# A graph network's second edge pass: ten steps of look-ahead, gathers gated by copy and scores; relation MLP with another order on TensorE

## What is computed

```
# layer 0, the relation MLP: for every edge
he = edge_attr @ edge_fc_W + edge_fc_b
t  = relu(einsum('ed,mdf->emf', he, rel_att_W1) + rel_att_b1)
g  = sigmoid(einsum('emf,mf->em', t, rel_att_W2) + rel_att_b2)

# layer 1, the second edge pass: src, dst per edge
e = tanh((X @ Wq)[src] + (X @ Wk)[dst])
scores = e @ Wphi
exp_scores = exp(scores - max(scores))
alpha = exp_scores / (segment_sum(exp_scores, src) + 1e-9)
msg = alpha * ((X @ Wy_w + Wy_b)[dst] + e @ We)
out = segment_sum(msg, src)
x = layernorm(x + out)
```

## Time and profile before

| | |
|---|---|
| median of the timed runs | 3582.48 us (3579.48 to 3582.94, 3 runs) |
| profiled execution | 3547.52 us, span 3545.2 us |
| granted TensorE clock, mean | 0.796 of full speed |
| busy share of the span: PE, DVE, POOL, ACT | 75%, 51%, 47%, 44% |
| relation MLP | 97 to about 669 us |
| first edge pass (unchanged) | about 800 to 1900 us |
| second edge pass: first gather, first and last `take` | 2084.5 us, 2142.2 us, 3471.5 us |

### The profile page before, as it was taken

One profiled execution on the slowest core, in us unless ns is written; L12 is line 12 of the kernel. 1 busy time (PEld: TensorE's weight loads), 2 busy tenths in 40 slices (PEclk: granted clock), 3 DMA queues, 4 the chain that ended last, 5 costly groups with the idle time before them and its releaser, 6 DMA issues. The chain is left out here.

```text
span 3545.2 us, 70863 instructions
## 1 busy us (share of the span) xinstructions
PE 2645.4 (75%) x17372; PEld 1828.1 (52%) x17372; DVE 1795.3 (51%) x5675; ACT 1560.4 (44%) x4560; POOL 1679.9 (47%) x1723
## 2 busy tenths in 40 slices
PE   5899999699877788887889545566666666676664
PEld 4343333277655566666667424455455455554552
DVE  8934531155433343334345625565565566565664
ACT  2677777455433333333335114344443444444442
POOL 0344444311356566655650035655656556666550
PEclk9999999889888778778779657766777767667775
DMA  8233333255433333333331022222222222222220
GB/s 96 90 100 98 98 108 110 65 180 147 137 107 104 97 99 102 99 101 98 102 95 60 14 68 59 66 63 62 70 62 67 65 62 66 66 67 67 63 59 18
DMA packets 321789, 297.77 MB, mean 84 GB/s; under 512 B 196992, under 2 KB 249237, under 8 KB 321680
## 3 DMA queue, kind: packets, MB, share of 16 engines
q0 software_dynamic: 72320, 160.26, 16.0%
q1 hardware_dynamic: 249360, 136.30, 13.9%
HBM read 191.89 MB, written 25.22 MB: 61 GB/s over the span
## 5 line engine op out<-in xcount | busy, mean ns | idle before, releaser
L1553 POOL DMA_INDIRECT sum_acc<-kv_table,rec_all x784 | 804.2, 1026 | 555.2 <-issue 207.5
L1043 POOL DMA_INDIRECT area_b<-h_table,src_g x544 | 559.8, 1029 | 370.6 <-remote 135.0
L1613 PE MATMUL bank<-sum_acc,probT 128*128 128x193 f32 x1760 | 506.8, 451 | 108.8 <-DVE probT L1741 57.8
L1613 PEld LDWEIGHTS bank<-sum_acc,probT 128*128 128x128 f32 x1760 | 416.2, 264 | 168.1 <-DVE probT L1741 89.6
L1113 PE MATMUL bank<-hs,y_sb 128*128 128x129 f32 x2400 | 415.9, 329 | 67.3 <-ACT y_sb L1136 64.5
L1113 PEld LDWEIGHTS bank<-hs,y_sb 128*128 128x128 f32 x2400 | 381.8, 241 | 79.6 <-ACT y_sb L1136 76.1
L501 POOL DMA_INDIRECT early<-h_table,src_g x240 | 236.9, 987 | 373.0 <-ACT sum_acc L707 290.3
L1140 ACT COPY y_sb<-bank 128x512 f32<-128x512 f32 x300 | 175.4, 585 | 520.1 <-PE bank L1104 282.9
L1227 DVE SCALAR_TENSOR_TENSOR sum_acc<-sum_acc,shrink,bank 128x129 f32 x300 | 104.7, 349 | 569.8 <-remote 266.6
L707 ACT ACTIVATE sum_acc<-bank,bias 128x512 f32<-128x512 f32 x588 | 351.4, 695 | 38.3 <-PE bank L585 30.9
L585 PE MATMUL bank<-area_b,wc 64*128 64x512 f32 x1176 | 362.1, 631 | 4.2 <-issue 3.7
(11 more groups left out here) (287 smaller groups left out, 4561.1 us busy)
## 6 DMA issues: line engine op xcount, KB each, us to landing
hs<-area_b SPq DMA_DIRECT2D x300, 258.0 KB
area_b<-in_edge_attr SPq DMA_DIRECT2D x97, 256.0 KB, 2.7
rows_table<-early POOLq DMA_DIRECT2D x60, 258.0 KB
area_b<-rows_table POOLq DMA_DIRECT2D x60, 258.0 KB
sum_acc<-kv_table,rec_all POOLq DMA_INDIRECT x784
qb<-q_table SPq DMA_DIRECT2D x220, 48.0 KB
area_b<-h_table,src_g POOLq DMA_INDIRECT x544
hbT<-hT_table SPq DMA_DIRECT2D x300, 16.0 KB
```

The costliest lines, as they stand in the source:

```text
L1043: pool.indirect_dma_start(out=landed_rows[:, k * GT + j, 0:D], out_offset=None, in_=h_table, in_offset=bass.IndirectOffsetOnAxis(ap=src_g[ ...
L1553: pool.indirect_dma_start(out=landed_rows[:, g % RING1 * GT + j, :], out_offset=None, in_=kv_table, in_offset=bass.IndirectOffsetOnAxis(ap ...
L1613: last = pe.matmul(bank[4 + k % 2][0:BN, 0:KV + 1], probT_v[:, k % 2, j, :], row_v[:, k % RING, j, AD:RK], start=(j == 0), stop=(j == GT - 1))
```

## The change

In the relation MLP `hidden(o)` becomes `hidden(o, m)`, a third of it, and PE and ACT take another order. In the second pass the look-aheads grow from 4 steps to 10, rings grow from 5 to 10 places (the rows of the ring now lie in three old buffers), two PSUM banks each take the transposes and the queries, and the four gathers of a group are issued in two pairs with a gate each. `SU` is 10, `PT` 5, `RING1` 8 as before. The core of the diff:

```diff
-RING = 5
+RING = 10
+PT = 5
...
-                    def hidden(o):
-                        pe.wait_ge(ea_sb, o + 1)
-                        for n in range(2 * M):
-                            m, half = n // 2, n % 2
+                    def hidden(o, m):
+                        if m == 0:
+                            pe.wait_ge(ea_sb, o + 1)
+                        for n in (2 * m, 2 * m + 1):
+                            half = n % 2
...
                     for o in range(OCTS):
-                        if o + 2 < OCTS:
-                            turn(o + 2)
                         if o + 1 < OCTS:
-                            hidden(o + 1)
+                            hidden(o + 1, 0)
+                            hidden(o + 1, 1)
+                        if o % 2:
+                            logits(o)
+                        elif o + 3 < OCTS:
+                            turn(o + 3)
+                        if o + 1 < OCTS:
+                            hidden(o + 1, 2)
+                        if o % 2 and o + 3 < OCTS:
+                            turn(o + 3)
                         if o >= TILE and o % TILE == 0:
                             turn_logits(o // TILE - 1)
-                        if o % 2:
-                            logits(o)
...
                     for o in range(OCTS):
-                        if o + 2 < OCTS:
-                            turned(o + 2)
                         if o >= TILE and o % TILE == 0:
                             keep_logits(o // TILE - 1)
                         if o + 1 < OCTS:
-                            rectified(o + 1)
+                            rectified(o + 1, (0, 1))
+                        if o % 2 == 0 and o + 3 < OCTS:
+                            turned(o + 3)
+                        if o + 1 < OCTS:
+                            rectified(o + 1, (2,))
+                        if o % 2 and o + 3 < OCTS:
+                            turned(o + 3)
...
-            row_v = area_a[:, 0:RING * GT * RK].rearrange("p (u j c) -> p u j c", u=RING, j=GT)
+            homes = [(area_a, RING1 * GT * KV + n * GT * RK) for n in range(6)] + [(x_words, n * GT * RK) for n in range(3)] + [(h_words, 0)]
+            row_v = [home[:, at:at + GT * RK].rearrange("p (j c) -> p j c", j=GT) for home, at in homes]
+            query_bank, hot_bank = (bank[0], bank[7]), (bank[1], bank[6])
...
                     def body(s, k, edge):
-                        if inside(edge, k, RING):
+                        if inside(edge, k, 7):
...
-                            sp.wait_ge(stepped, n + 1)
+                            sp.wait_ge(sum_done, n + 1)
                             load_step(s1, k1, g, b)
...
-                    pool.memset(row_v[:, :, :, KV + AD:RK], 1.0).then_inc(cleared, 1)
+                    for row in row_v:
+                        pool.memset(row[:, :, KV + AD:RK], 1.0).then_inc(cleared, 1)
...
-                            pool.wait_ge(stepped, last_step + SU + 1)
-                        gather(g)
+                            pool.wait_ge(moved, last_step + 1)
+                        gather(g, 0)
+                        if g >= RING1:
+                            pool.wait_ge(score_done, last_step + 1)
+                        gather(g, 1)
...
                     def body(s, k, edge):
-                        if inside(edge, k, 1):
-                            share_top(*step_of(s, k, 1))
                         if inside(edge, k, 3):
-                            queries(*step_of(s, k, 3))
-                        if inside(edge, k, 4):
-                            turn(*step_of(s, k, 4))
-                        if inside(edge, k, 2):
-                            turn_max(*step_of(s, k, 2))
+                            share_top(*step_of(s, k, 3))
+                        if inside(edge, k, 7):
+                            queries(*step_of(s, k, 7))
+                        if inside(edge, k, 9):
+                            turn(*step_of(s, k, 9))
                         if inside(edge, k, 1):
                             messages(*step_of(s, k, 1))
-                    rounds(pe, body, 4)
+                        if inside(edge, k, 5):
+                            turn_max(*step_of(s, k, 5))
+                    rounds(pe, body, 9)
...
                     def body(s, k, edge):
-                        if inside(edge, k, 3):
-                            move_rows(*step_of(s, k, 3))
                         if inside(edge, k, 2):
-                            tanh(*step_of(s, k, 2))
-                        if inside(edge, k, 4):
-                            squared(*step_of(s, k, 4))
-                        if inside(edge, k, 1):
-                            exponentials(*step_of(s, k, 1))
-                        if inside(edge, k, 4):
-                            turned(*step_of(s, k, 4))
-                    rounds(act, body, 4)
+                            exponentials(*step_of(s, k, 2))
+                        if inside(edge, k, 8):
+                            turned(*step_of(s, k, 8))
+                        if inside(edge, k, 6):
+                            tanh(*step_of(s, k, 6))
+                        if inside(edge, k, 7):
+                            move_rows(*step_of(s, k, 7))
+                        if inside(edge, k, 10):
+                            squared(*step_of(s, k, 10))
+                    rounds(act, body, 10)
...
                     def body(s, k, edge):
+                        if inside(edge, k, 6):
+                            add_queries(*step_of(s, k, 6))
+                        if inside(edge, k, 4):
+                            highest(*step_of(s, k, 4))
+                        if inside(edge, k, 9):
+                            outside(*step_of(s, k, 9))
+                        if inside(edge, k, 10):
+                            hot(*step_of(s, k, 10))
+                        if inside(edge, k, 6):
+                            score(*step_of(s, k, 6))
                         if inside(edge, k, 2):
-                            add_queries(*step_of(s, k, 2))
-                        if inside(edge, k, 3):
-                            outside(*step_of(s, k, 3))
-                        if inside(edge, k, 4):
-                            hot(*step_of(s, k, 4))
-                        if inside(edge, k, 1):
-                            highest(*step_of(s, k, 1))
-                        if inside(edge, k, 2):
-                            score(*step_of(s, k, 2))
-                        if inside(edge, k, 1):
-                            spread_p(*step_of(s, k, 1))
+                            spread_p(*step_of(s, k, 2))
                         if inside(edge, k, 0):
                             take(s, k)
-                    rounds(v, body, 4)
+                    rounds(v, body, 10)
```

More of the change, by code:

```diff
@@ L699, in keep_logits, with rectified @@
                         act.activation(logit, bank[5][:, :], ACT.Identity, bias=bias2[:, 0:1]).then_inc(logit_sb, 1)
-                    def rectified(o):
-                        if o >= 3:
+                    def rectified(o, pairs):
+                        if o >= 3 and 0 in pairs:
                             act.wait_ge(logit_ps, (o - 3) // 2 + 1)
-                        for n in range(2 * M):
+                        for n in range(2 * pairs[0], 2 * pairs[-1] + 2):
                             m = n // 2
@@ L725, in _ @@
                     turned(1)
-                    rectified(0)
+                    rectified(0, (0, 1, 2))
+                    turned(2)
                     for o in range(OCTS):
-                        if o + 2 < OCTS:
-                            turned(o + 2)
                         if o >= TILE and o % TILE == 0:
@@ L1541, in body, with gather @@
                             tell(s, k)
-                    sp.wait_ge(cleared, 1)
-                    rounds(sp, body, RING)
+                    sp.wait_ge(cleared, RING)
+                    rounds(sp, body, 7)
                 @block.gpsimd
                 def _(pool):
-                    pool.memset(row_v[:, :, :, KV + AD:RK], 1.0).then_inc(cleared, 1)
+                    for row in row_v:
+                        pool.memset(row[:, :, KV + AD:RK], 1.0).then_inc(cleared, 1)
                     pool.memset(acc_st, 0.0).then_inc(cleared, 1)
                     pool.memset(top_st, NONE).then_inc(cleared, 1)
-                    def gather(g):
+                    def gather(g, pair):
                         pool.sem_inc(ticks, 1)
-                        for j in range(GT):
+                        for j in (2 * pair, 2 * pair + 1):
                             pool.indirect_dma_start(
@@ L1578, in turn @@
                         n = s * SU + k
-                        if not is_first(n):
-                            pe.wait_ge(hotT_done, n)
+                        into = hot_bank[k % 2][0:BN, :].bitcast(BF16)
+                        pe.wait_ge(hotT_done, n + 1)
```

(4 more changed lines are left out.)

92 lines of the change are left out of this document (51 added, 41 removed).

## The result

The changed kernel takes 3630.54 us (median of four runs, 3625.8 to 3637.05), beside 3582.71 us for the kernel before on the same chip (3579.48 to 3584.41): ratio 1.0147, interval 1.012 to 1.0174. It is 48 us slower. The forecast was 204 us faster: 3378 us, in a range of 3280 to 3495 us. The measured time lies 135 us above that range.

A forecast was written before the change was run, and what follows sets the result against it. The prediction took PE's late hand-over during gather chains as the second pass's bound. Steps -195, clearings +3 and MLP -12 gave -204 us: 3378 us as median from 3582.5, range 3280 to 3495 us.

The forecast's parts named there:

- What bounds the step: Second edge pass: PE's results are announced late while POOL chains gathers, making a step 6.07 us.
- rival 1: Second pass: lateness wholly hidden, POOL gathers without pause, 4.73 us per step, 3280 us in all; chance 0.17.
- the gates stay shut and the chain ends: Second pass: when PE is held, ACT and DVE soon have nothing to copy or score, so POOL's gathers stop.
- rival 3: Second pass: gates open earlier, POOL never pauses for PE, 7.05 us per step, +215 us, 3780 us; chance 0.08.
- the pace by a chain of four: Second pass: four gathers, 5.3 us, pace 196 of 220 steps; 5.18 us per step on average, -195 us.
- Rival 4: Second pass: no effect, lateness grows with the look-ahead, 6.05 us per step, within 0.2%; chance 0.03.
- the other terms: Outside the second pass's steps: +3 us for more clearings of ones columns on POOL, -12 us for the relation MLP.
- Fill: Start of the second pass: three more short bodies, some 9 us, offset by a shorter end; counted 0, up to 10 us either way.
- what is queued behind a late load: SP in the second pass: `tell`, on which `move_rows` waits, has a 10 us window against 7.5 us lateness; counted 0.
- MLP: Relation MLP: ACT idles 2.59 us, not 2.72, per pair, and logit turns fall behind its work; -12 us, bounds 0 and -60.
- Gathers beside DVE: Second pass: denser DVE work lengthens gathers, mean over median from 79 to some 92 ns; -184 us instead of -195.
- the clock: PE in the second pass: denser work keeps PE at the upper clock level more often; no size given.

The follow-up runs named there:

- gate on PE: The changed kernel with its gathers also waiting for PE's queries and messages: 3491.08 us where before took 3570.28, one run each; 0.9903 where before took 2952.6.
- old gate: The changed kernel with all four gathers of a group waiting again for PE's messages: 2923.53 us, ratio 0.9898, where before took 2951.89 us.
- new gate: The kernel before with only the gathers' waits changed to ACT's copy and DVE's scores: 2954.68 us, ratio 1.0005, where before took 2951.89 us.
- MLP part alone: The kernel before with only the new order of PE's and ACT's work in the relation MLP: 2923.51 us, ratio 0.9908.

## Why the prediction was wrong, by its steps

**What bounds the step: right for this chip, taken for a property of the kernel.** The late hand-over of PE during a chain of gathers is what the first chip shows, before and after. Five other chips don't show it. There the step is POOL's own 4.63 to 4.71 us, which is the step of rival 1 (4.73), but rings and gates are worth nothing, since the kernel before is at that floor too.

**The step that failed: "the gates stay shut and the chain ends".** This was the argument that kept rival 3 at 0.08, and the pace by a chain of four (5.18 us) rests on it: after four gathers POOL was to wait for the next score. But each score opens the gate for four more gathers, DVE's steps are 4.1 us apart, and four gathers take 5.1 us, so the next gate is open before the four are out. DVE makes that score from PE results of the body before, and the chain doesn't end until DVE has used up what it has. In the stall above the scores end at 2899.39 and 2903.57 us (`lane_max`), which let out the gathers from 2900.18 and from 2905.30 us, eight in one chain:

```profile
2899.31 0.08 DVE L1762 DVE_READ_ACCUMULATOR2_ANT lane_max<- 128x1 f32 x1
...
2903.49 0.08 DVE L1762 DVE_READ_ACCUMULATOR2_ANT lane_max<- 128x1 f32 x1
...
2905.30 0.95 POOL L1573 DMA_INDIRECT sum_acc<-kv_table,rec_all  x1 [0.30 <-issue]
```

DVE stops at 2905.2 us and waits for PE until 2911.98. So the forecast's argument isn't false in itself, DVE does run dry, but too late: the gate for four more gathers was opened 1.6 us before. PE's first gap comes only at 2906.2 us. It is so in most chains of eight and more behind the fill, 64 in all: in 37 of them no score ends after PE's first unexplained gap over 0.9 us, in 3 there is no such gap, and in 24 DVE goes on to score while PE is held. The chains grew from four and eight to eight and twelve, and the wait for PE with them. In the kernel before, the gate waited for PE's own messages, and I read it as a brake, though a loose one (39 chains of eight): POOL could not go far where PE was held. It was taken away in the same edit that gave the slack to hide lateness. It is rival 3 in kind, and in size 6.34 us, not 7.05: the loop of two bodies meets its lateness in one step of three (74 of 219), not in each.

What the runs show of this: chains, steps and waits in the three traces of chips that hold PE, and that beside the gate on PE, in one run, the chains are shorter and the step is 5.78 us. What they don't show: the old gate and the new gate each alone there. So that one run puts the brake, with the look-ahead kept, at 0.56 us per step; how much of the loss comes from the gates and how much from the rings stays open.

Two slips in the forecast's numbers changed nothing of this. Rival 3's own terms give 3582.5 + 215 + 3 - 12 = 3788 us and not 3780. Rival 4's 6.05 us per step is 4 us for the pass, and with the 9 us of the other terms 0.4%, not "within 0.2%".

**Fill, counted 0, was +36 us.** The forecast saw that SP has to be seven bodies ahead and named `tell` as what is queued behind a late load, and priced it at nothing. In the fill ACT's first copy came at 2122.14 us, when the 32 gathers' chain was over, and what it waited for is SP's `tell` (L1549). SP's loads of records and q rows and ACT's copy in the timeline:

```profile
2091.30 0.01 SPq L1543 DMA_DIRECT2D qb<-q_table  x1
2100.49 0.71 SPq L1542 DMA_DIRECT2D rec_sb<-rec  x1
2104.69 0.70 SPq L1543 DMA_DIRECT2D qb<-q_table  x1
2120.79 0.00 SPq L1542 DMA_DIRECT2D rec_sb<-rec  x1
2120.89 0.33 SPq L1543 DMA_DIRECT2D qb<-q_table  x1
2122.14 0.83 ACT L1668 COPY sum_acc<-sum_acc 128x768 f32 x1 [40.90 <-SPq L1549]
```

Two loads of a step are 0.5 us apart at the start of the fill (2072.65 and 2073.19 us); under the chain one load takes SP 4, 9 and 16 us. SP has the loads of eight steps ahead of its first `tell` (it runs seven bodies ahead), and had those of six: the sixth step's record load was issued at 2101.55 us in before, and ACT's copy came at 2105.97. So the two more steps, at the pace of a held SP, moved the first copy from 21.5 to 46.5 us behind the first gather, 25 of the 36 us; the other 11 us are in the six short bodies ahead of the first `take`, that the forecast put at 9 us. On free chips, where SP isn't held, the fill grows by 17 us (26.7 us in the new gate's kernel, 43.9 in after). The forecast set its 9 us off against a shorter end. What comes behind the last `take` is as long as before (72.9 us, 73.7 before). On free chips, where the gathers pace the pass, the longer fill costs nothing, and on the chip that holds no such return is seen. The count of loads was not changed by itself in a run.

**MLP: the mechanism right, sized 12 us, measured 26.** ACT's wait moved to the fifth hidden bank, as forecast; two of those places, and the logits ahead of the first:

```profile
416.26 2.78 PE L598 MATMUL bank<-sum_acc,w_shift 128*32 128x512 f32 x24
...
420.14 1.26 ACT L716 ACTIVATE sum_acc<-bank,bias 128x512 f32<-128x512 f32 x2 [2.15 <-PE bank L587]
...
431.70 1.27 ACT L716 ACTIVATE sum_acc<-bank,bias 128x512 f32<-128x512 f32 x2 [1.29 <-PE bank L587]
```

The waits of ACT from 97 to 643 us:

```profile
ACT sum_acc L716 <- PE bank L587: 125.8, 63, 5.1
...
ACT area_b L702 <- PE bank L576: 1.2, 1, 1.2
```

That is 127.0 / 49 = 2.59 us per pair of octets, the forecast's figure. What was mis-sized is before: I took its idle time from one pair (2.72 us), and its waits for PE from 97 to 669 us are 109.8 + 30.9 us, 2.87 us per pair. So waits for PE gave 13.7 us of the 26 by which the stretch is shorter, about the 12 forecast; ACT's busy time, 415.0 us before and 408.9 after for the same 743 recorded instructions, gave 6, and its other waits 2.6 us (13.2 to 10.6). The last 4 us are in gaps that neither view lists. On free chips the last hidden product starts at 634.9 us against 662.4, 27.5 us, and the MLP part alone is worth 28 us, so this term holds on both kinds of chip.

**The first pass, not in the sum, +16 us.** The unchanged first pass took 927 us before and 943 after on the chip that holds, and 708 and 711 us on free ones (921.1 to 1629.1 in the new gate's kernel, 890.5 to 1601.3 in after). It is a stretch where POOL waits for "remote" too, on the chip that holds alone (135 us in before, 152 in after). Whether the 16 us are of the change or of the execution is open.

**Gathers beside DVE, and the clock.** The longer gathers of the forecast did not come: the mean lies 23 ns above the median (972 and 949 ns), where it was 79 ns (1026 and 947), and DVE did not get denser, its busy share fell from 60 to 55%. On the free chip DVE is busy 76% of the steps, and the difference is 78 ns (1024 and 946). So it doesn't grow with DVE's busy share as the forecast scaled it. The rule that it was scaled from (the Trainium skill, SBUF — State Buffer, section "SBUF: two separate sides", on the port pair that DVE and GpSimd share) is neither borne out nor denied by this. The clock stayed at 0.72 (0.73 before), so nothing was shown on it.

**What is best.** The gate on PE beats before wherever it ran: 0.9903 [0.9887, 0.992] on a free chip, 0.978 in one run on a chip that holds. On free chips it equals after (0.9907); on one that holds it took 3491 us where after took 3631. Until that run is repeated, its gain there is not an established figure. Of the other kernels those with the new MLP order are equal to it on free chips and, after aside, unmeasured on the others.

## What to carry to other kernels

A wait that looks like the bottleneck can be a brake. Ask, before it is replaced by a signal that comes earlier, what the waiting engine will do with its freedom, and whom that holds up. When slack is added so that lateness can be hidden, check whether the cause of the lateness is fed by the same slack. And before a wait without a record of its releaser is priced as the kernel's own, run the kernel unchanged on a second chip.

## What the runs showed of the hardware that was not expected

The kernel before takes 3570 to 3583 us in two comparisons and 2951 to 2954 us on five other chips, with the same instructions. Where it is slow, other engines are held while POOL issues indirect gathers back to back. A set of eight matmuls stretches from 1.5 us to 7.4 us, in single ones some 2 us apart. A finished result of PE reaches DVE 8.9 us later. A register operation of SP takes up to 1407 ns for a median of 43 ns; ACT's and DVE's take up to 729 and 712 ns in after, and POOL's don't grow (147 ns as the median, 151 as the longest, in L1584). Where the kernel is fast a chain of all 784 gathers does nothing of the kind (52 ns at most on SP).

The MLP ends within 8 us on both kinds (last hidden product of after at 642.8 and 634.9 us), and the stretch between the passes, without gathers, within 1 us. The first pass takes 927 us on one kind, 708 on the other. The granted clock differs too, 0.72 and 0.81 in the steps of after, and PE is busy 816 and 706 us there. But the steps last 1389 and 1015 us, and PE is not the bound in either, so the clock is no more than a part of it.

What sets the kind, the chip or what else runs beside it, is open: the runs can't tell.
